# A graph layer with an FFN: half of the FFN up product moved into the first bucket's sums, half between the down products

## The chip, the cores and the metric

One core of one Trainium2 chip. The metric is the device time in microseconds of one execution, the median of several runs. The kernel is written instruction by instruction: each engine has its own program, and semaphores order them against each other.

## The reference

6250 nodes with 256 features (fp32) and 106250 edges. In short:

```
xn = layernorm(x)
low  = relu(segment_sum(val_low[:, None]  * (xn @ W_low)[src],  dst))
high = relu(segment_sum(val_high[:, None] * (xn @ W_high)[src], dst))
mlp  = relu(xn @ W_mlp)
att  = softmax(sigmoid([low @ a0, high @ a1, mlp @ a2]) @ A / 3)
x1   = x + 3 * (att0 * low + att1 * high + att2 * mlp) + mix(xn)
x2   = layernorm(x1)
w    = x2 @ wr + br
y    = gelu(x2 @ w1 + b1) @ w2 + b2        # 256 -> 1024 -> 256
out  = x1 + x2 + (w is among the top 3124) * w * y
```

The kernel sums the node features over the edges first and multiplies by the weights W_low and W_high afterwards. `mix` is a linear attention with an MLP; it is done before the part that the change touches.

## The kernel before, in words

Up to about 850 us of the trace the kernel sorts the edges by target node, stores the normalized rows in memory and does the mix part. Then comes the loop that matters here, in `pipeline`: 50 stages over T = 49 tiles of 128 nodes, written out (not a loop on the chip). A tile has two buckets of 64 nodes. The sorted edges lie in columns of 128; a column's 128 source rows (256 fp32 each, 128 KB) are gathered from memory by one indirect DMA that GpSimd issues (L665), into a ring of 32 columns (`gring`). There are 852 columns, some 8.7 for a bucket.

A bucket's sums are matmuls on TensorE: `bucket` takes ten columns, five in a first half and five in a second, and in between, by a branch, the extra columns of a bucket that spans more. The stationary operand `msel` is a selection matrix of 128 x 128 that VectorE builds for each half (L1116 and L1122 in `select`), and the moving one is the gathered column (128x256), whose place in the ring is computed at run time. After each half TensorE increments `sel_used`. SyncE waits for `sel_used` values (L562) and frees the ring's columns in groups of 8 (`col_free`, L564); GpSimd issues the gathers of a group when it is freed.

In stage i TensorE works on several tiles at once (function `stage` of the tensor block), in this order: transposes of the sums of tile i-1 (L1817), the bias of the down product of tile i-3, transposes of the normalized tile i-2 (L1827), the product with the two GNN weights for tile i-1, the first bucket of tile i into bank 0, down for tile i-3 (eight matmuls of 128x256 into bank 7, then `y_psum`), up for tile i-2 (sixteen of 128x128, banks 4 and 5, `f1_psum` after each eight), and the second bucket of tile i into bank 1. Nearly all matmuls are recorded at L1528, the helper `mm`. An fp32 matmul of the source appears as two weight loads and two matmuls in the trace.

The other engines in a stage. ScalarE: the copy of bank 1 (L1443, releases the next stage's transposes), the copies of the transposes (L1447), the GNN product (L1452), the transposed tile (L1456, sets `x2t_ready`), then the copy of bank 0 (L1490), which waits for the second half of the first bucket, then the attention (L1460, L1462), the reciprocal square root, the scaling of y (L1481, waits for `y_psum`) and the gelus (L1438, wait for `f1_psum`). VectorE, in its program's order: the end of tile i-2, the selection matrices of the first bucket, the attention and layer norm of tile i-1 (`post_a`, L1164 to L1197), and only then the selection matrices of the second bucket. `post_a` waits for the attention's first tanh on ScalarE (L1460), which stands behind L1490:

```
if here:
    act.wait_ge(S("sel_used"), 4 * i + 2)
    act.activation(agg[:, 0, :], bank[0][:, 0:D], ACT.Copy).then_inc(S("agg_a"), 1)
if before1:
    attention(i)
```

Of the kernel before, what the change touches and what calls it, by code (L numbers as in the profile page):

```python
# [22 lines left out]
P = 128  # L23
# [27 lines left out]
def build(nc, a, out):  # L51
# [6 lines left out]
    KD = D // P  # L58
# [40 lines left out]
    with ExitStack() as ctx:  # L99
        sems = {}  # L100

        def S(name):
            if name not in sems:
                sems[name] = ctx.enter_context(nc.semaphore(name))
            return sems[name]
# [1420 lines left out]
        def _(pe):  # L1526
            def mm(out_, lhsT, rhs, start, stop, **kw):
                return pe.matmul(out_, lhsT, rhs, start=start, stop=stop, **kw)  # L1528
# [241 lines left out]
            def add_col(acc, weights, col, start, stop):  # L1770

                at = pe.snap((col % GR) * D)
                return mm(acc[:, 0:D], weights, rows[:, ds(at, D)], start, stop, skip_group_check=True)

            def bucket(b, acc):

                word = bucket_word(pe, b)
                lo = first_col(pe, word)
                more = extra_cols(pe, word)
                pe.wait_ge(S("g_ready"), pe.snap(lo + VIS))  # L1780
                pe.wait_ge(S("sel_ready"), 2 * b + 1)
                for j in range(VIS):
                    ins = add_col(acc, msel[:, 2 * b % NBUF, j, :], lo + j, j == 0, False)
                ins.then_inc(S("sel_used"), 1)
                with pe.If(more > 0):
                    done = extras_so_far(pe, b)
                    with pe.Fori(0, more) as e:
                        pe.wait_ge(S("g_ready"), pe.snap(lo + e + VIS + 1))
                        pe.wait_ge(S("sel_x_ready"), pe.snap(done + e + 1))
                        add_col(acc, msel_x[:, :], lo + e + VIS, False, False).then_inc(S("sel_x_used"), 1)  # L1790
                rest = pe.snap(lo + more)
                pe.wait_ge(S("g_ready"), pe.snap(rest + BOTH))
                pe.wait_ge(S("sel_ready"), 2 * b + 2)
                for j in range(VIS):
                    ins = add_col(acc, msel[:, (2 * b + 1) % NBUF, j, :], rest + VIS + j, False, j == VIS - 1)
                ins.then_inc(S("sel_used"), 1)

            def up(part):

                for f in range(part * KF // 2, (part + 1) * KF // 2):  # L1800
                    for k in range(KD):
                        ins = mm(bank[4 + part][:, (f % 4) * P:(f % 4 + 1) * P], w1f[:, k, f * P:(f + 1) * P], x2t[:, k, :],
                                 k == 0, k == KD - 1)
                return ins

            def down(lo, hi):

# [4 lines left out]
            def stage(i, here, before1, before2, before3):  # L1812
# [24 lines left out]
                    ins.then_inc(S("lh_psum"), 1)  # L1837
                if here:
                    wait(pe, S("agg_a"), i)
                    bucket(2 * i, bank[0])  # L1840
                if before3:
                    down(0, KF).then_inc(S("y_psum"), 1)
                if before2:
                    if isinstance(i, int) and i == 2:
                        pe.wait_ge(S("ffn_loaded"), 16 * 2)
                    pe.wait_ge(S("x2t_ready"), i - 1)
                    for part in range(2):
                        up(part).then_inc(S("f1_psum"), 1)
                if here:
                    wait(pe, S("agg_b"), i)  # L1850
                    bucket(2 * i + 1, bank[1])
# [11 lines left out]
            def end():  # L1863
# [7 lines left out]
                down(0, KF).then_inc(S("y_psum"), 1)  # L1871
                count_total(0)
                pe.wait_ge(S("x2t_ready"), T)
                up(0).then_inc(S("f1_psum"), 1)
                count_total(1)
                up(1).then_inc(S("f1_psum"), 1)
                count_total(2)
                down_bias(T - 1)
                pe.wait_ge(S("fh_ready"), T * KF)
# [36 lines left out]
```

## Time and profile before

| | |
|---|---|
| median of 3 runs | 2526.34 us |
| lowest, highest run | 2504.72, 2528.77 us |
| span of the profiled execution | 2481.7 us |
| its own time around the span | not on the page |
| TensorE busy | 1719.4 us, 69% of the span |
| GpSimd, VectorE, ScalarE busy | 1371.7, 1229.1, 924.8 us |
| gathers from the node rows (L665) | 852 |

The page has the busy time by engine, the span in 40 slices, the DMA queues, the chain of work that ended last, and the costliest groups of instructions by line. Below it the trace answers for single stretches: a timeline has one row for a run of like instructions, with its start, its length, how many, and the idle time before it with what ended that. "issue" stands for no releaser known, "remote" for one that the profile cannot name. Four stages of the loop are looked at, each from its L1817 transposes to the next one's: stage A from 1476.31 us, B from 1384.57, C from 1535.19, D from 2299.98.

### The profile page before, as it was taken

To read this page: it belongs to the slowest core of one execution; us is meant where nothing else is said; L and a number is where in the kernel's file an instruction comes from. 1 tells how busy PE (TensorE), PEld (TensorE's weight loads), DVE (VectorE), ACT (ScalarE), POOL (GpSimd) and SP (SyncE) were. 2 spreads that over 40 slices of the span, in tenths; PEclk is the share of its full clock that TensorE was granted. 3 is DMA by queue.
4 is the path that set the end of the run, shared out by engine and by line. 5 is a ranking of instruction groups with operands and counts; after the bars stand their busy time and mean duration, and the time that the engine had idled before them with its cause. 6 is when DMAs were issued, how large, how long until landed. Compare 5 with 4: busy or idle time off the path is not lost.

```text
span 2481.7 us, 30518 instructions
## 1 busy us (share of the span) xinstructions
PE 1719.4 (69%) x9109; PEld 1441.9 (58%) x9109; DVE 1229.1 (50%) x3164; ACT 924.8 (37%) x2641; POOL 1371.7 (55%) x1351
## 2 busy tenths in 40 slices
PE   4788884998865347776777677677577677667672
PEld 4566673887754335665665666566466566556562
DVE  8899995888761223432343333333333333333336
ACT  2677873777652112321222222222222222222223
POOL 3277675788776565545555455455455545554600
PEclk9899996999967667888887888788788788788886
DMA  3221211111100422222222222222222222222303
GB/s 90 72 63 54 80 33 30 46 54 46 46 5 5 133 85 72 78 69 75 71 74 71 68 73 75 65 72 75 68 73 75 75 69 71 81 71 68 85 9 104
DMA packets 102212, 162.99 MB, mean 66 GB/s; under 512 B 32190, under 2 KB 72762, under 8 KB 102040
## 3 DMA queue, kind: packets, MB, share of 16 engines
q0 software_dynamic: 55232, 113.59, 16.4%
q1 hardware_dynamic: 46808, 47.29, 6.0%
q8 instruction: 85, 1.39, 0.2%
q14 instruction: 87, 0.71, 0.1%
HBM read 139.76 MB, written 21.04 MB: 65 GB/s over the span
## 4 chain that ended last, share of the span: by engine, by line
PE 51%; issue 23%; DVE 10%; ACT 9%; another core or an unknown queue 5%; DMA 1%; SPq 1%; POOL 0%; DVEq 0%; ACTq 0%; POOLq 0%
PE bank L1528 49%; ACT side L1303 2%; PE bank L1817 1%; ACT base L1303 1%; ACT arena L1303 1%; DVE arena L811 1%; ACT arena L1447 1%; ACT arena L1443 1%; DVE arena L733 1%; ACT side L1519 1%; DVE arena L766 1%; ACT arena L1307 0%; PE bank L1602 0%; DVE arena L781 0%
## 5 line engine op out<-in xcount | busy, mean ns | idle before, releaser
L1528 PE MATMUL bank<-arena 128*128 128x128 f32 (+3 forms) x6320 | 1292.5, 359 | 508.2 <-issue 426.8
L1528 PEld LDWEIGHTS bank<-arena 128*128 128x128 f32 (+1 forms) x6320 | 1094.8, 205 | 683.8 <-issue 500.0
L665 POOL DMA_INDIRECT arena<-xn_rows,arena x852 | 825.5, 969 | 733.8 <-SPq L564 450.0
L648 POOL DMA_INDIRECT sorted_records<-arena x448 | 523.0, 1167 | 256.0 <-issue 139.3
L1167 DVE CUSTOM_DVE_ANT_0 arena<-arena 128x256 f32<-128x256 f32 x98 | 37.8, 423 | 414.9 <-ACT arena L1452 376.1
L1122 DVE TENSOR_TENSOR arena<-arena 128x640 f32<-128x640 bf16 (+1 forms) x204 | 164.2, 805 | 47.6 <-DVE arena L1116 17.7
L1172 DVE SCALAR_TENSOR_TENSOR att_prod<-sg,att_neg 128x9 f32<-128x9 f32 x49 | 8.5, 174 | 334.9 <-issue 300.8
L1490 ACT ACTIVATE arena<-bank 128x256 f32<-128x256 f32 x49 | 18.8, 383 | 355.5 <-remote 262.1
L1116 DVE SCALAR_TENSOR_TENSOR arena<-io,arena 128x320 bf16<-128x320 f32 (+1 forms) x204 | 97.8, 479 | 106.3 <-DVE wall L1209 43.5
L1528 PE MATMUL bank<-arena,base 128*128 128x128 f32 (+3 forms) x766 | 118.4, 287 | 16.7 <-ACT base L1307 8.3
L1438 ACT ACTIVATE arena<-bank,b1f 128x128 f32<-128x128 f32 x392 | 110.3, 372 | 33.5 <-PE bank L1528 28.1
L811 DVE TENSOR_TENSOR arena<-arena 128x1280 f32<-128x1280 bf16 x84 | 120.5, 1488 | 4.1 <-remote 1.7
L1528 PEld LDWEIGHTS bank<-arena,base 128*128 128x128 f32 (+2 forms) x766 | 110.2, 211 | 17.6 <-ACT base L1307 8.5
L1443 ACT ACTIVATE arena<-bank 128x256 f32<-128x256 f32 x49 | 18.8, 383 | 247.0 <-PE bank L1528 219.3
L1528 PE MATMUL bank<-side,arena 128*128 128x512 f32 x196 | 97.1, 619 | 0.3 <-issue 0.3
L1481 ACT ACTIVATE side<-bank,wall 128x256 f32<-128x256 f32 x49 | 23.1, 472 | 176.0 <-remote 165.3
L1303 ACT ACTIVATE base<-arena 128x128 f32<-128x128 f32 x280 | 84.7, 391 | 9.4 <-DVE arena L792 9.4
L1468 ACT ACTIVATE nr<-nri 128x1 f32<-128x1 f32 x49 | 9.9, 203 | 206.0 <-issue 159.8
L1303 ACT ACTIVATE arena<-arena 128x128 f32<-128x128 f32 x280 | 84.6, 397 | 0.0
L1303 ACT ACTIVATE side<-arena 128x128 f32<-128x128 f32 x280 | 84.6, 392 | 0.0
L1528 PE MATMUL bank<-arena,side 128*128 128x128 f32 x560 | 73.5, 282 | 12.0 <-issue 10.9
L1528 PEld LDWEIGHTS bank<-arena,side 128*128 128x128 f32 x560 | 68.0, 196 | 15.6 <-issue 14.1
(312 smaller groups left out, 1889.2 us busy)
## 6 DMA issues: line engine op xcount, KB each, us to landing
arena<-xn_rows,arena POOLq DMA_INDIRECT x852
sorted_records<-arena POOLq DMA_INDIRECT x448
arena<-in_x SPq DMA_DIRECT2D x12, 512.0 KB
xn_rows<-arena SPq DMA_DIRECT2D x12, 512.0 KB
x_plus_xn_rows<-arena SPq DMA_DIRECT2D x12, 512.0 KB
arena<-x_plus_xn_rows SPq DMA_DIRECT2D x12, 512.0 KB
arena<-xn_rows SPq DMA_DIRECT2D x12, 512.0 KB
out<-base SPq DMA_DIRECT2D x4, 1024.0 KB
```

Of the source, the lines that this page charges most:

```text
L648: pool.indirect_dma_start(rec_dram, bass.IndirectOffsetOnAxis(ap=idx[0:PR, par, u:u + 1], axis=0), stage_rec[0:PR, par, u * 8:(u + 1) * 8] ...
L665: pool.indirect_dma_start(gring[:, c % GR, :], None, xn_dram, bass.IndirectOffsetOnAxis(ap=rring[:, c, 3:4].bitcast(I32), axis=0)).then_in ...
L733: ins = dve.tensor_tensor(oh[:, t, :].rearrange("p j (h e) -> p j h e", e=2), twice[:, t, :].unsqueeze(2).to_broadcast([P, GS, NB // 2, 2] ...
L766: dve.tensor_tensor(prod4[:, :, :, 0:NB], oh[:, :, :].rearrange("p (s j) b -> p s j b", s=GROUPS), rankf[:, :].rearrange("p (s b) -> p s b ...
L811: dve.tensor_tensor(cellrec[:, t, :].rearrange("p t (f c) -> p t f c", f=4), cell[:, t, :].unsqueeze(2).to_broadcast([P, GS, 4, GC]), raw[ ...
L1116: return dve.scalar_tensor_tensor(out_, io64[:, :].unsqueeze(1).to_broadcast([P, n, BK]), float(BK * b), r[:, :, 0:1].to_broadcast([P, n, ...
L1122: return dve.tensor_tensor(out_, hots.unsqueeze(2).to_broadcast([P, n, 2, BK]), r[:, :, 1:3].unsqueeze(3).to_broadcast([P, n, 2, BK]), ALU ...
L1167: ins = dve.tensor_tensor_reduce(out=lg_prod[:, k, :], in0=lh[:, k * D:(k + 1) * D], in1=att_rows[:, k, :], scale=1.0, scalar=0.0, op0=ALU ...
L1303: ins = act.activation(quot[:, j, :], iota32[:, :], ACT.Abs, bias=p32[:, par, s * GS + j:s * GS + j + 1], scale=-1.0)
L1438: act.activation(fh[:, f, :], bank[4 + part][:, (f % 4) * P:(f % 4 + 1) * P], ACT.Gelu_apprx_tanh, bias=b1f[:, f:f + 1]).then_inc(S("fh_re ...
L1443: act.activation(agg[:, 1, :], bank[1][:, 0:D], ACT.Copy).then_inc(S("agg_b"), 1)
L1528: return pe.matmul(out_, lhsT, rhs, start=start, stop=stop, **kw)
```

## The change

The up product of a stage is cut into blocks: `up_block(f)` is the two matmuls of the hidden block f, and after every fourth it increments `f1_psum`. Blocks 0 to 3 are issued inside the second half of the first bucket, one ahead of each of its first four columns. The waits for the transposed tile (and, in stage 2, for the FFN weights) stand ahead of them, in the bucket. Blocks 4 to 7 alternate with the eight matmuls of down: a block, two of down, and so on. `y_psum` still comes after the last of down. In the stages without a bucket (the last one) all blocks alternate with down. The last tile's end is the same but for where `f1_psum` is written down in the source.

```
             def bucket(b, acc, turned=0):
...
                 pe.wait_ge(S("sel_ready"), 2 * b + 2)
+                if turned == 1:
+                    pe.wait_ge(S("ffn_loaded"), 16 * 2)
+                if turned:
+                    pe.wait_ge(S("x2t_ready"), turned)
                 for j in range(VIS):
+                    if turned and j < KF // 2:
+                        up_block(j)
                     ins = add_col(acc, msel[:, (2 * b + 1) % NBUF, j, :], rest + VIS + j, False, j == VIS - 1)
                 ins.then_inc(S("sel_used"), 1)

+            def up_block(f):
+
+                for k in range(KD):
+                    ins = mm(bank[4 + f // 4][:, (f % 4) * P:(f % 4 + 1) * P], w1f[:, k, f * P:(f + 1) * P], x2t[:, k, :],
+                             k == 0, k == KD - 1)
+                if f % 4 == 3:
+                    ins.then_inc(S("f1_psum"), 1)
...
                 if here:
                     wait(pe, S("agg_a"), i)
-                    bucket(2 * i, bank[0])
+                    bucket(2 * i, bank[0], i - 1 if before2 else 0)
+                elif before2:
+                    pe.wait_ge(S("x2t_ready"), i - 1)
+                for f in range(KF):
+                    if before2 and (not here or f % 2 == 0):
+                        up_block(KF // 2 + f // 2 if here else f)
+                    if before3:
+                        ins = down(f, f + 1)
                 if before3:
-                    down(0, KF).then_inc(S("y_psum"), 1)
-                if before2:
-                    if isinstance(i, int) and i == 2:
-                        pe.wait_ge(S("ffn_loaded"), 16 * 2)
-                    pe.wait_ge(S("x2t_ready"), i - 1)
-                    for part in range(2):
-                        up(part).then_inc(S("f1_psum"), 1)
+                    ins.then_inc(S("y_psum"), 1)
```

How TensorE's row changes, from the second half of the first bucket on, in a middle stage (bank0: the first bucket's sums, bank7: down, bank4 and bank5: up, ISA: the register work for a column's place). Before:

```order
L1792 ISA
L1528 ISA [waits sel_ready,g_ready]
L1528 MATMUL bank0<-arena 128x256
L1528 ISA
L1528 MATMUL bank0<-arena 128x256
L1528 ISA
L1528 MATMUL bank0<-arena 128x256
L1528 ISA
L1528 MATMUL bank0<-arena 128x256
L1528 ISA
L1528 MATMUL bank0<-arena 128x256
L1528 MATMUL bank7<-arena 128x256 x8
```

and now:

```order
L1792 ISA
L1528 MATMUL bank4<-arena 128x128 [waits x2t_ready,sel_ready,g_ready]
L1528 MATMUL bank4<-arena 128x128
L1528 ISA
L1528 MATMUL bank0<-arena 128x256
L1528 MATMUL bank4<-arena 128x128 x2
L1528 ISA
L1528 MATMUL bank0<-arena 128x256
L1528 MATMUL bank4<-arena 128x128 x2
L1528 ISA
L1528 MATMUL bank0<-arena 128x256
L1528 MATMUL bank4<-arena 128x128 x2
```

The eight short matmuls into bank 4 now stand between the columns of bank 0, so the last column's matmul, which increments `sel_used`, has them ahead of it.

Then the row up to the second bucket (TENSOR_LOAD of `packed` is its first instruction). Before:

```order
L1528 MATMUL bank0<-arena 128x256
L1528 MATMUL bank7<-arena 128x256 x8
L1528 MATMUL bank4<-arena 128x128 [waits x2t_ready]
L1528 MATMUL bank4<-arena 128x128 x7
L1528 MATMUL bank5<-arena 128x128 x8
L406 TENSOR_LOAD packed [waits agg_b]
```

and now:

```order
L1528 ISA
L1528 MATMUL bank0<-arena 128x256
L1528 MATMUL bank5<-arena 128x128 x2
L1528 MATMUL bank7<-arena 128x256 x2
L1528 MATMUL bank5<-arena 128x128 x2
L1528 MATMUL bank7<-arena 128x256 x2
L1528 MATMUL bank5<-arena 128x128 x2
L1528 MATMUL bank7<-arena 128x256 x2
L1528 MATMUL bank5<-arena 128x128 x2
L1528 MATMUL bank7<-arena 128x256 x2
L406 TENSOR_LOAD packed [waits agg_b]
```

The down products into bank 7 come later by the short ones between them, and the last instructions ahead of the second bucket are two of down, not eight of up.

## Rows read from the trace of the kernel before

**Rows 1.** The page: busy time by engine, and the chain that ended last.

```profile
PE 1719.4 (69%) x9109; PEld 1441.9 (58%) x9109; DVE 1229.1 (50%) x3164; ACT 924.8 (37%) x2641; POOL 1371.7 (55%) x1351
...
PE 51%; issue 23%; DVE 10%; ACT 9%; another core or an unknown queue 5%; DMA 1%; SPq 1%; POOL 0%; DVEq 0%; ACTq 0%; POOLq 0%
```

**Rows 2.** Waits from 1100 to 2300 us: us in total, times, longest us.

```profile
POOL arena L665 <- SPq L564: 371.7, 53, 13.1
...
PE bank L1528 <- issue: 326.4, 247, 3.2
...
ACT arena L1490 <- remote: 194.7, 24, 11.1
```

**Rows 3.** Groups by shape from 1100 to 2300 us: busy us, mean ns, idle before.

```profile
L1528 PE MATMUL bank<-arena 128*128 128x128 f32 x1216 | 236.3, 328 | 328.1 <-issue 324.9 <-DVE arena L1122 2.5
```

**Rows 4.** Timeline of TensorE in stage A: start us, length us, records, idle before.

```profile
1476.31 0.66 PE L1817 MATMUL bank<-ident,arena 128*128 128x128 f32 x4 [0.47 <-ACT arena L1443]
...
1477.72 11.95 PE L1528 MATMUL bank<-arena 128*128 128x256 f32 x61 [0.42 <-ACT arena L1447]
1490.40 0.40 PE L1528 MATMUL bank<-arena 128*128 128x128 f32 x2 [0.73 <-issue]
...
1497.55 6.98 PE L1528 MATMUL bank<-arena 128*128 128x128 f32 x29 [0.38 <-issue]
```

**Rows 5.** Timeline of GpSimd around stage A.

```profile
1474.65 0.94 POOL L665 DMA_INDIRECT arena<-xn_rows,arena  x1 [9.12 <-SPq L564]
...
1485.56 0.94 POOL L665 DMA_INDIRECT arena<-xn_rows,arena  x1 [1.09 <-issue]
...
1494.43 0.95 POOL L665 DMA_INDIRECT arena<-xn_rows,arena  x1 [0.30 <-issue]
```

**Rows 6.** Stage D, timelines of TensorE, GpSimd, ScalarE and VectorE.

```profile
2301.39 13.34 PE L1528 MATMUL bank<-arena 128*128 128x256 f32 x76 [0.42 <-ACT arena L1447]
2319.27 6.27 PE L1528 MATMUL bank<-arena 128*128 x20 [4.55 <-DVE arena L1122]
2326.01 0.66 PE L1817 MATMUL bank<-ident,arena 128*128 128x128 f32 x4 [0.47 <-ACT arena L1443]
...
2309.24 0.94 POOL L665 DMA_INDIRECT arena<-xn_rows,arena  x1 [1.10 <-issue]
2311.85 0.94 POOL L665 DMA_INDIRECT arena<-xn_rows,arena  x1 [1.67 <-issue]
...
2311.21 0.38 ACT L1490 ACTIVATE arena<-bank 128x256 f32<-128x256 f32 x1 [6.92 <-remote]
...
2318.08 0.88 DVE L1122 TENSOR_TENSOR arena<-arena 128x640 f32<-128x640 bf16 x1
```

**Rows 7.** Stretches: stage A, stage C, stage D (us, then busy us and count by engine).

```profile
1476.31:1505.00 28.69, 21.87 (x103) 18.47 (x104) 11.29 (x37) 7.98 (x26) 14.95 (x16) 0.88 0.26 75
1535.19:1575.93 40.74, 23.65 (x104) 19.67 (x104) 11.52 (x37) 7.98 (x26) 22.00 (x23) 0.75 0.27 78
2299.98:2326.01 26.03, 20.59 (x104) 17.65 (x104) 11.43 (x37) 7.76 (x26) 15.26 (x17) 0.93 0.29 82
```

**Rows 8.** Timeline of ScalarE: L1490 and L1481 in stage A, and L1490 in C.

```profile
1488.99 0.38 ACT L1490 ACTIVATE arena<-bank 128x256 f32<-128x256 f32 x1 [8.37 <-remote]
...
1497.71 0.47 ACT L1481 ACTIVATE side<-bank,wall 128x256 f32<-128x256 f32 x1 [0.25 <-remote]
...
1550.63 0.38 ACT L1490 ACTIVATE arena<-bank 128x256 f32<-128x256 f32 x1 [11.13 <-remote]
```

**Rows 9.** Records of L1528 started in A and in C until L1490 started.

```profile
1477.60:1488.95 11.35, 11.21 (x57) 9.89 (x58) 1.00 0.36 102
1536.50:1550.58 14.08, 11.66 (x58) 10.15 (x58) 1.00 0.37 106
```

**Rows 10.** Stage B: ScalarE's copy, and GpSimd's ninth gather.

```profile
1393.64 0.38 ACT L1490 ACTIVATE arena<-bank 128x256 f32<-128x256 f32 x1 [4.77 <-PE bank L1528]
...
1395.18 0.94 POOL L665 DMA_INDIRECT arena<-xn_rows,arena  x1 [0.30 <-issue]
```

More of the change, by code:

```diff
@@ L1773, in add_col, with bucket @@
                 return mm(acc[:, 0:D], weights, rows[:, ds(at, D)], start, stop, skip_group_check=True)
-            def bucket(b, acc):
+            def bucket(b, acc, turned=0):
                 word = bucket_word(pe, b)
@@ L1793, in bucket @@
                 pe.wait_ge(S("sel_ready"), 2 * b + 2)
+                if turned == 1:
+                    pe.wait_ge(S("ffn_loaded"), 16 * 2)
+                if turned:
+                    pe.wait_ge(S("x2t_ready"), turned)
                 for j in range(VIS):
+                    if turned and j < KF // 2:
+                        up_block(j)
                     ins = add_col(acc, msel[:, (2 * b + 1) % NBUF, j, :], rest + VIS + j, False, j == VIS - 1)
                 ins.then_inc(S("sel_used"), 1)
+            def up_block(f):
[4 more added lines that the diff above has]
+                    ins.then_inc(S("f1_psum"), 1)
             def up(part):
                 for f in range(part * KF // 2, (part + 1) * KF // 2):
[L1801 to L1804, printed above, removed]
+                    up_block(f)
             def down(lo, hi):
@@ L1873, in end @@
                 pe.wait_ge(S("x2t_ready"), T)
-                up(0).then_inc(S("f1_psum"), 1)
+                up(0)
                 count_total(1)
-                up(1).then_inc(S("f1_psum"), 1)
+                up(1)
                 count_total(2)
```

## The prediction

> **What bounds the kernel now.** I read the page first [rows 1]: TensorE is busy 69% of the span, but 23% of the chain that ended last is "issue", time in which an engine waited for nothing the profile names. Then the waits of the 1,200 us stretch 1100 to 2300 us, which holds some 38 stages of the loop over node tiles [rows 2]: TensorE stands 326.4 us on "issue", in 247 pieces, while GpSimd, which issues the gathers, waits 371.7 us for SyncE's releases. Then the groups by shape [rows 3]: nearly all of TensorE's 326.4 us stand in front of the 128x128 matmuls, the FFN up product, in which the program has no wait after the first. So the place that the change touches is the place where the engine stands.
>
> Why does it stand there? I took single stages. One record of a weight load with one of a matmul I call a pair; each fp32 matmul of the source is two pairs. A stage has 7 small ones (four transposes, the bias, two transposes), then 96 pairs: 8 of the product with the GNN weights, 10 and 10 of the first bucket's two halves, 16 of down, 32 of up, 20 of the second bucket. In stage A (1476.31 to 1505.00) 61 of the 96 start in one run, then six trickle in over some 7 us, and the last 29 run again from 1497.55 [rows 4]. GpSimd's gathers of this stage run from 1474.65 to 1495.38 (1494.43 + 0.95), 16 of them, one each 1.25 us, with a break of 1.09 us after the eighth [rows 5]. TensorE comes free 2.2 us after the last of them. In stage D the gathers had a break at 2310.2 to 2311.85; TensorE ran 76 pairs without a stop, and the stage took 26.0 us instead of 28.7 [rows 6, 7].
>
> The messages of TensorE tell more. The copy of the first bucket's sums (ScalarE L1490) waits for the second half's last matmul, pair 28; in the stretch it waits 194.7 us for a releaser that the profile can't name ("remote") [rows 2]. That pair starts some 7.3 us into a stage (1.4 us, and 27 times 0.22), yet L1490 starts at 1488.99 in stage A (12.7 us in) and at 1550.63 in stage C (15.4 us in) [rows 8]. I counted what TensorE had started by then: 57 matmuls and 58 weight loads in A, 58 and 58 in C [rows 9], though the two moments are 2.7 us apart in their stages. So while gathers run, the completion of a pair is reported only when about 30 further pairs have started: completions leave in order, one for each instruction, and slowly. The scaling of the down product (L1481) says the same: it waits for pair 44, which starts at 10.8 us in, and starts at 1497.71, just after TensorE came free [rows 8]. In stage D, with the break, L1490 starts 1.0 us after the gather before the break ended [rows 6]. Why the completions are held is not in the trace; that they are, and in which order, is.
>
> The second thing to see is what hangs on L1490. It is followed by the attention, VectorE's chain for the tile and only then VectorE's selection matrices for the second bucket, since VectorE keeps its program order. In stage D: L1490 at 2311.21, selection ready at 2318.96, second bucket from 2319.27 [rows 6]: 8.1 us. From there 6.7 us to the next stage's transposes (2326.01). So where this chain decides, a stage ends 14.8 us after L1490 (20 pairs in 6.27 us is the rate at a granted clock near 1.2 GHz, TensorE having stood; at 0.22 us each, as in the run of 76, it would be 1.9 less). In stage A this chain needs 1497.1, and TensorE comes to the second bucket at some 1499.4: hidden, by 2.3 us.
>
> **The change, part by part.** Instructions are neither added nor taken away: the same 32 up pairs, moved; no DMA, no other engine's code. (a) Half of up, 16 pairs, goes into the second half of the first bucket. The wait for the transposed tile moves ahead of it; that copy lands 3.9 us into a stage, and the half begins at 5.3: nothing. (b) The other half stands between the down pairs. Pure order, except for what stands behind TensorE's release: of the 8 pairs then left, 4 are now of 256 columns instead of 128. At 6.27 us for 20 such pairs [rows 6] that is 0.31 each, 0.16 more than a half-wide one, 0.6 us a stage. (c) The message that L1490 waits for now sits on pair 44 instead of 28. Without any hold that is 16 short pairs later, 1.8 us (13.34 us for 76 pairs of which 32 are half as wide [rows 6]: 0.22 us for a wide one, 0.11 for a short one). With the hold it is the whole matter: pair 44 is where the down product's message sat, and that one never came through before the gathers ended. By the count, TensorE would have to start 74 pairs for it, and it has 67 when it is released (96 less the 29 of the last run [rows 4]).
>
> So L1490 moves to the end of the gathers, or to their first break. There are four kinds of stage among the 45 from the third on. A stage begins with its four transposes (L1817); the counts are from the timeline of GpSimd's gathers, by the number in a burst, its start in the stage and what released each group of 8:
> - 23 like A: both groups released by earlier halves. L1490 at 21.2 after the stage's start (1497.55 less 1476.31), stage 21.2 + 14.8 = 36.0. Before, their mean is 29.2 (A 28.7 [rows 7]): +6.8 each, +156.
> - 4 with the same releases but gathers from 0.5 to 20.6 in: L1490 at 23.4, stage 38.2 against 30.9: +29.
> - 11 like B: the second group of 8 is released by this very message (L1490 at 1393.64, the ninth gather at 1395.18 [rows 10]). Now GpSimd runs dry at 10.5 in, the break lets the completions out as in stage D, after 1.0 us, or 2.2 as at a burst's end; I take 1.6, near the middle. L1490 at 12.1, stage 26.9 against 31.0: -4.1 each, -45.
> - 7 like C: 24 gathers, the last 8 released by this message. The break comes at 18.4, L1490 at 20.6, stage 35.4 against 40.7 [rows 7]: -5.3 each, -37.
>
> Sum: 156 + 29 - 45 - 37 = +103 us on the profiled execution's span of 2481.7. Its own time around the span isn't on the page; the lowest of the three runs, 2504.72, is 23 above it, the median 44.6. I add the difference to the median: 2526 + 103 = 2629, say 2630. (b) isn't added, since TensorE then waits for VectorE anyway. Bounds of the uncertain terms: if pair 44's message came as early as pair 28's plus 1.8 us, the first two kinds cost 0.6 us each or +17; if the two dry kinds save nothing, the sum is +185; if the second bucket ran at the quick rate in the 27 slower stages, it is 51 less, +52.
>
> On the hold itself a page speaks against me. The Trainium skill, "SBUF — State Buffer", section "SBUF: two separate sides", says that engine ports and DMA ports are disjoint and that a DMA can't be slowed by a compute operation or the other way round. By that rule the gathers wouldn't hold TensorE, the message would move by 1.8 us alone, and the sum would be that of the first rival; the break of stage D and TensorE's release 2.2 us after the gathers speak for a link, if not through these ports.
>
> **Rivals.**
> First: the message moves with its instruction, by some 2 us, and nothing more. Then L1490 is at 14.5 in stage A, the second bucket could start at 22.6, where TensorE arrives at 23.1: still hidden, and only (b) is paid: 45 x 0.6 = 27 us, 2553. For it: in B and stages like it, pair 28's message came within 2 us. Against it: 58 pairs in both A and C, and the down message, which was never early.
> Second, on the other side: the dry GpSimd wins. In the 18 stages of the last two kinds the break is worth 82 us; if in the other 27 the message of pair 44 comes by about 15 us into the stage (15 + 8.1 is where TensorE arrives now), these lose only 0.6 us each. 2526 - 82 + 17 = 2461. It decides on whether pair 44 can be reported before some 62 pairs have started. For it: the break after the eighth gather in A did come while completions were held; against it: pair 28 had been done by then and still wasn't reported until 1488.99.
> Third: the interleaving evens out TensorE's rate and the hold never builds up. Then all stages go like D, near 27: 45 stages at a mean of 31.6 before would give some 2320. Against it: the number of pairs is the same, and the run of 61 ended in the same place in stages whose gathers began 2 us apart.
>
> **Chances.** The forecast 0.52. First rival 0.20, at +27 us just on the border of 1% (1% is about what a measurement of this kernel can tell from no change), so half of it counts as the same. Second 0.19, third 0.04, the rest (a mixture that cancels, near zero) 0.05. Faster 0.24, same 0.16, slower 0.60. The range leaves the third rival and the very worst out: 2455 to 2700.
>
> **What would show it.** In the changed kernel's trace: L1490 starting 20 us and more into most stages, just after TensorE's release, where L1481 starts now; the second bucket waiting for VectorE L1122 by some 5 us, a wait that the profile then names; TensorE's "issue" time about as large as before in stages like A, and gone in stages like B, which shrink to 27; stages like C at 35. Wrong, if L1490 starts at 13 to 15 in stages like A: then the count of 30 pairs is no rule. Wrong the other way, if more than 70 pairs start before the gathers end.

## The result: slower, and the profile after

The changed kernel takes 2622.22 us in the median (2607.58 to 2635.47, four runs); the kernel before 2527.56 (2504.72 to 2559.39, four runs, three of them those of the table above). The ratio is 1.0483, with a 95% interval from 1.0438 to 1.0527. Two further sets of the unaltered changed kernel gave 1.0468 and 1.0438 (below). Where several runs of a kernel lie in two groups, the ratios and intervals here and below are those of the faster group, so that they can differ from the quotient of the medians.

The page of the profiled execution (2607.58 us, span 2605.8), the busy times and the chain that ended last, which answer to [rows 1]:

```profile
PE 1785.5 (69%) x9109; PEld 1446.8 (56%) x9109; DVE 1230.7 (47%) x3164; ACT 915.3 (35%) x2641; POOL 1378.3 (53%) x1351
...
PE 34%; another core or an unknown queue 21%; issue 14%; DVE 13%; POOL 9%; ACT 7%; DVEq 1%; DMA 1%; SPq 0%; ACTq 0%; POOLq 0%
```

The counts are the same on every engine. The chain has shifted: TensorE from 51% to 34%, "issue" from 23% to 14%, and "another core or an unknown queue", which is what the profile writes for a message that it can't attribute, from 5% to 21%. Two groups of the page say which message. Before:

```profile
L1172 DVE SCALAR_TENSOR_TENSOR att_prod<-sg,att_neg 128x9 f32<-128x9 f32 x49 | 8.5, 174 | 334.9 <-issue 300.8
...
L1490 ACT ACTIVATE arena<-bank 128x256 f32<-128x256 f32 x49 | 18.8, 383 | 355.5 <-remote 262.1
```

and now:

```profile
L1172 DVE SCALAR_TENSOR_TENSOR att_prod<-sg,att_neg 128x9 f32<-128x9 f32 x49 | 8.3, 170 | 647.1 <-ACT sg L1460 586.2
L1490 ACT ACTIVATE arena<-bank 128x256 f32<-128x256 f32 x49 | 18.8, 383 | 677.4 <-remote 667.7
```

ScalarE stands 677.4 us in front of the copy of the first bucket (355.5 before), and VectorE 647.1 us for the attention behind it (334.9): 49 copies of 0.38 us are what the stage waits for. The waits of the stretch 1100 to 2400 us (us in total, times, longest us), which answer to [rows 2]; it is 100 us longer than the stretch there, and holds as many stages, some 38:

```profile
ACT arena L1490 <- remote: 532.3, 38, 19.0
DVE att_prod L1172 <- ACT sg L1460: 474.4, 33, 18.9
...
PE bank L1528 <- issue: 226.4, 200, 6.0
...
PE bank L1528 <- DVE arena L1122: 136.7, 23, 7.0
```

The wait for the unnamed releaser went from 194.7 us in 24 pieces to 532.3 in 38. TensorE's "issue" became smaller, 326.4 to 226.4, and beside it there is now a wait with a name, 136.7 us for VectorE's L1122, the selection matrices of the second bucket; it was 2.5 us [rows 3]. TensorE still stands inside its own products, but less, and now it also waits for the chain.

A stage like A, from 1548.68 to 1585.75. TensorE, then ScalarE, then GpSimd, as timelines (start us, length us, records, idle before); they answer to [rows 4, 5 and 8]:

```profile
1548.68 0.66 PE L1828 MATMUL bank<-ident,arena 128*128 128x128 f32 x4 [0.47 <-ACT arena L1443]
...
1550.08 11.05 PE L1528 MATMUL bank<-arena 128*128 128x256 f32 x63 [0.42 <-issue]
...
1568.21 3.06 PE L1528 MATMUL bank<-arena 128*128 128x128 f32 x6 [0.34 <-issue]
1577.65 7.63 PE L1528 MATMUL bank<-arena 128*128 x20 [6.37 <-DVE arena L1122]
1585.75 0.66 PE L1828 MATMUL bank<-ident,arena 128*128 128x128 f32 x4 [0.47 <-ACT arena L1443]
```

```profile
1569.66 0.38 ACT L1490 ACTIVATE arena<-bank 128x256 f32<-128x256 f32 x1 [16.67 <-remote]
```

```profile
1554.65 0.94 POOL L665 DMA_INDIRECT arena<-xn_rows,arena  x1 [0.30 <-SPq L564]
...
1565.90 0.95 POOL L665 DMA_INDIRECT arena<-xn_rows,arena  x1 [0.30 <-issue]
1583.24 1.35 POOL L665 DMA_INDIRECT arena<-xn_rows,arena  x1 [16.39 <-SPq L564]
```

63 pairs in one run, a trickle while the gathers go on, the last gather done at 1566.85, TensorE free at 1568.21, the copy at 1569.66, 21.0 us after the stage's start. From the copy 8.0 us to the second bucket, and TensorE has stood 6.37 us by then. GpSimd in turn stands 16.39 us, since its columns are freed by the same halves.

A stage like B, from 1446.31 to 1473.87, which answers to [rows 10]:

```profile
1447.71 13.34 PE L1528 MATMUL bank<-arena 128*128 128x256 f32 x76 [0.42 <-ACT arena L1447]
1466.52 6.88 PE L1528 MATMUL bank<-arena 128*128 x20 [5.47 <-issue]
...
1458.34 0.38 ACT L1490 ACTIVATE arena<-bank 128x256 f32<-128x256 f32 x1 [7.72 <-remote]
...
1455.67 0.94 POOL L665 DMA_INDIRECT arena<-xn_rows,arena  x1 [0.30 <-issue]
1459.27 0.94 POOL L665 DMA_INDIRECT arena<-xn_rows,arena  x1 [2.65 <-SPq L564]
```

Here GpSimd runs dry at 1456.61, 10.3 us in; the copy comes 1.7 us later, and TensorE runs 76 pairs without a stop. The three kinds as stretches (length us; busy us and count of PE, PEld, DVE, ACT, POOL; granted clock; DMA share; GB/s), against [rows 7]:

```profile
1446.30:1473.91 27.61, 21.24 (x104) 17.98 (x104) 11.57 (x37) 7.76 (x26) 15.93 (x16) 0.88 0.28 77
1548.70:1585.70 37.00, 24.55 (x103) 19.31 (x103) 11.29 (x37) 7.76 (x26) 15.23 (x16) 0.77 0.21 60
1623.30:1658.80 35.50, 23.68 (x103) 18.92 (x104) 11.48 (x37) 7.76 (x26) 22.20 (x23) 0.76 0.30 87
```

The 45 stages together: from the third stage's transposes to the 48th's, in the kernel before and in the changed one:

```profile
945.45 0.66 PE L1817 MATMUL bank<-ident,arena 128*128 128x128 f32 x4 [0.47 <-ACT arena L1443]
...
2367.28 0.66 PE L1817 MATMUL bank<-ident,arena 128*128 128x128 f32 x4 [0.47 <-ACT arena L1443]
```

```profile
961.96 0.66 PE L1828 MATMUL bank<-ident,arena 128*128 128x128 f32 x4 [0.47 <-ACT arena L1443]
...
2483.86 0.66 PE L1828 MATMUL bank<-ident,arena 128*128 128x128 f32 x4 [0.47 <-ACT arena L1443]
```

1421.8 us before, 1521.9 now: +100.1. The rest of the difference of the two spans, 24 us, lies outside these stages. 18.1 of it has come together by the loop's first transposes (889.91 us before, 908.04 now), where the change moves nothing. 7.6 lies behind the 48th stage's transposes (114.4 to 122.0 us), where the last stages and the last tile still carry the change. The first two stages are 1.6 us shorter.

### The profile page after: what moved, and what is told of

It reads as the page before. It is cut to its first block, busy times and chain, and to the rows that moved or that the text cites. A ratio compares the mean times of both kernels' runs of the same rounds, so it can differ in the third digit from the quotient of the medians.

```text
span 2605.8 us, 30518 instructions
## 1 busy us (share of the span) xinstructions
PE 1785.5 (69%) x9109; PEld 1446.8 (56%) x9109; DVE 1230.7 (47%) x3164; ACT 915.3 (35%) x2641; POOL 1378.3 (53%) x1351
## 3 DMA queue, kind: packets, MB, share of 16 engines
q0 software_dynamic: 55232, 113.59, 15.7%
## 4 chain that ended last, share of the span: by engine, by line
PE 34%; another core or an unknown queue 21%; issue 14%; DVE 13%; POOL 9%; ACT 7%; DVEq 1%; DMA 1%; SPq 0%; ACTq 0%; POOLq 0%
PE bank L1528 32%; POOL sorted_records L648 9%; PE bank L1828 1%; DVE arena L1122 1%; ACT arena L1443 1%; ACT arena L1452 1%; ACT side L1519 1%; ACT arena L1447 1%; DVE arena L1116 1%; DVE arena L811 1%; DVE arena L1189 1%; DVE ybuf L1187 1%; DVE arena L1186 1%; ACT side L1303 1%
## 5 line engine op out<-in xcount | busy, mean ns | idle before, releaser
L1528 PE MATMUL bank<-arena 128*128 128x128 f32 (+3 forms) x6320 | 1359.1, 370 | 559.0 <-issue 312.5
L1528 PEld LDWEIGHTS bank<-arena 128*128 128x128 f32 (+1 forms) x6320 | 1100.2, 207 | 798.9 <-issue 604.5
L665 POOL DMA_INDIRECT arena<-xn_rows,arena x852 | 833.9, 979 | 828.1 <-SPq L564 553.0
L1172 DVE SCALAR_TENSOR_TENSOR att_prod<-sg,att_neg 128x9 f32<-128x9 f32 x49 | 8.3, 170 | 647.1 <-ACT sg L1460 586.2
L1490 ACT ACTIVATE arena<-bank 128x256 f32<-128x256 f32 x49 | 18.8, 383 | 677.4 <-remote 667.7
L1122 DVE TENSOR_TENSOR arena<-arena 128x640 f32<-128x640 bf16 (+1 forms) x204 | 164.0, 804 | 31.8 <-DVE arena L1116 3.2
L1528 PE MATMUL bank<-arena,base 128*128 128x128 f32 (+3 forms) x766 | 116.8, 285 | 26.0 <-ACT base L1307 17.0
L1528 PEld LDWEIGHTS bank<-arena,base 128*128 128x128 f32 (+2 forms) x766 | 108.7, 209 | 26.7 <-ACT base L1307 17.5
L1528 PE MATMUL bank<-side,arena 128*128 128x512 f32 x196 | 97.5, 621 | 0.3 <-issue 0.3
L1528 PE MATMUL bank<-arena,side 128*128 128x128 f32 x560 | 74.1, 283 | 12.7 <-issue 12.3
L1528 PEld LDWEIGHTS bank<-arena,side 128*128 128x128 f32 x560 | 68.8, 198 | 15.2 <-issue 14.8
L766 DVE TENSOR_TENSOR arena<-arena 128x2940 f16<-128x2940 bf16 x28 | 47.3, 1689 | 58.5 <-issue 46.4
```

The costliest lines, as they stand in the source:

```text
L665: pool.indirect_dma_start(gring[:, c % GR, :], None, xn_dram, bass.IndirectOffsetOnAxis(ap=rring[:, c, 3:4].bitcast(I32), axis=0)).then_in ...
L766: dve.tensor_tensor(prod4[:, :, :, 0:NB], oh[:, :, :].rearrange("p (s j) b -> p s j b", s=GROUPS), rankf[:, :].rearrange("p (s b) -> p s b ...
L1122: return dve.tensor_tensor(out_, hots.unsqueeze(2).to_broadcast([P, n, 2, BK]), r[:, :, 1:3].unsqueeze(3).to_broadcast([P, n, 2, BK]), ALU ...
```

## The experiments

Eight kernels of my own, two of them run twice, and the changed kernel two times more. The first four ran beside the same 14 runs of the kernel before.

### One half of the move at a time

`e1_bucket_half_only` keeps blocks 0 to 3 inside the bucket and puts down back in one piece, the other blocks behind it:

```
                 for f in range(KF):
-                    if before2 and (not here or f % 2 == 0):
-                        up_block(KF // 2 + f // 2 if here else f)
-                    if before3:
-                        ins = down(f, f + 1)
...
+                    ins = down(0, KF)
                     ins.then_inc(S("y_psum"), 1)
+                if before2:
+                    for f in range(KF // 2 if here else 0, KF):
+                        up_block(f)
```

> Half of up inside the first bucket as in the changed kernel, the other half behind down as before. Theory (the message of pair 44 leaves only when the gathers stop, and the stage ends 14.8 us after it): this half alone is the whole loss, 2600 to 2640 us, L1490 about 21 us into stages like A. Rival (the interleaving of up with down, or of short and wide matmuls, costs): near 2530.

Measured: 2605.81 us (2585.84 to 2653.16), the kernel before beside it 2507.95 (14 runs): 1.0367, interval 1.0279 to 1.0456. The waits of 1100 to 2400 us:

```profile
ACT arena L1490 <- remote: 533.8, 38, 19.0
...
PE bank L1528 <- DVE arena L1122: 150.8, 23, 7.4
```

The wait at L1490 is that of the whole change, 533.8 against 532.3 us. The half in the bucket alone makes the long stages, as expected.

`e2_down_half_only` is the other half: nothing in the bucket, blocks 0 to 3 right behind it, then the alternation with down.

```
-                    bucket(2 * i, bank[0], i - 1 if before2 else 0)
+                    bucket(2 * i, bank[0])
...
+                    if here:
+                        for f in range(KF // 2):
+                            up_block(f)
```

> Nothing inside the bucket: the first half of up behind it, the second half between the down products. Theory: L1490 keeps pair 28 and starts at about 12.7 us in stages like A, stages as long as before, 2520 to 2560 us. Rival (interleaving costs): 2580 and more.

Measured: 2530.51 us (2515.44 to 2539.74): 1.0129, interval 1.0066 to 1.0193. A stage of the kind of A:

```profile
1480.65 10.35 PE L1528 MATMUL bank<-arena 128*128 128x256 f32 x57 [0.42 <-ACT arena L1447]
...
1498.99 9.91 PE L1528 MATMUL bank<-arena 128*128 128x256 f32 x30 [0.83 <-issue]
1509.37 0.66 PE L1822 MATMUL bank<-ident,arena 128*128 128x128 f32 x4 [0.47 <-ACT arena L1443]
...
1491.88 0.38 ACT L1490 ACTIVATE arena<-bank 128x256 f32<-128x256 f32 x1 [8.33 <-remote]
```

L1490 comes 12.6 us into the stage (12.7 in stage A before), but what is left when TensorE is released, 30 pairs with wide ones among them, takes 9.91 us where it took 6.98 for 29 [rows 4]. Over the 45 stages it is 1454.7 us, 32.9 more than before, 0.7 a stage. That is near the 0.6 a stage of the prediction's part (b), but in this stage it isn't made of part (b)'s wide pairs alone: the run of 30 went at a granted clock of 0.66, the 29 of stage A at 0.79, and it began 19.8 us into the stage, not 21.2. So the alternation costs little, as forecast; that the four wide pairs are what it costs isn't shown.

### How far the message may move

`e3_one_block` leaves one block in the bucket, `e4_two_blocks` two; the others stand behind down. The message that L1490 waits for is then on pair 32 and on pair 36, after 28 in the kernel before and 44 in the changed one.

```
-                    if turned and j < KF // 2:
+                    if turned and j < 1:
```

> One block (4 pairs) inside the bucket, seven behind down: the message is on pair 32. Theory: it leaves when about 62 pairs have started, some 13.3 us in, which is still hidden; 2520 to 2560 us. Rival (anything between the columns costs in proportion to its pairs): a quarter of the loss, 2550.

> Two blocks (8 pairs) inside the bucket: the message is on pair 36. Theory: it needs some 66 started pairs and so leaves just before or at the end of the gathers in stages like A, 18 to 21 us in; most of the loss is there already, 2570 to 2620 us. Rival (in proportion): half of the loss, 2575. The place of L1490 tells them apart: at 18 to 21 against 13 to 15 us.

Measured: e3 2519.59 us (2468.62 to 2549.33, ten runs), 0.9945, interval 0.9867 to 1.0024. e4 2528.22 us (2487.48 to 2584.41, four runs), for which there is no interval: no verdict, though its slowest run is still below the fastest of the changed kernel's in any set, 2594.67. The 2570 to 2620 expected of e4 was wrong, and for the rival's 2575 there is no sign either. Their profiled executions took 2549.28 and 2531.61 us, so only what happens within their stages is read from them. The copy in a stage of the kind of A of e3, and the run of TensorE around it:

```profile
1272.10 0.38 ACT L1490 ACTIVATE arena<-bank 128x256 f32<-128x256 f32 x1 [9.83 <-remote]
...
1259.37 11.86 PE L1528 MATMUL bank<-arena 128*128 128x256 f32 x61 [0.42 <-ACT arena L1447]
```

and in e4:

```profile
1295.94 0.39 ACT L1490 ACTIVATE arena<-bank 128x256 f32<-128x256 f32 x1 [11.90 <-remote]
...
1304.10 6.05 PE L1528 MATMUL bank<-arena 128*128 x20 [1.99 <-DVE arena L1122]
```

The stages begin at 1257.97 and 1279.73. So the copy comes 12.7 us into such a stage with the message on pair 28, 14.1 on 32, 16.2 on 36, 21.0 on 44: 1.4 us for the first four pairs, 2.1 for the next four, 4.8 for the last eight. Sixteen pairs more at the rate of the free run, 0.175 us a pair, would be 2.8 us; they are 8.3. And it is not steady: of the 23 stages of this kind, five in e3 and nine in e4 have their copy at 19.6 to 21.2 us, and in the changed kernel 21 of them at 20.6 to 22.3. The later the message stands, the more often it falls behind the last gather. The expectation for e4, the copy at 18 to 21 us in stages like A, so holds for fewer than half of them. In e4, 10 of the 45 stages are of 27.0 to 27.7 us, those in which GpSimd runs dry, which pays for some of the long ones.

One number is the same in all four places of the message. Over the 45 stages of each kernel, at most 59 pairs had started when the copy did with the message on pair 28, 63 with it on pair 32, 67 on 36 and 75 on 44: 31 behind it each time.

### Does a break in the gathers let the completions out?

The next four kernels were made for that. `e5` and `e6` are the changed kernel and the one before with a single edit in SyncE's program, which rounds the count of used passes up to an even number, so that groups of 8 are freed later:

```
-                        used = sp.snap(word % 256, min_val=1, max_val=255)
+                        used = sp.snap((word % 256 + 1) // 2 * 2, min_val=2, max_val=256)
```

`e7` is e6, and SyncE also waits until TensorE has come to the up product of a stage (its first matmul increments `paced`; in the first two stages, which have no up product, the first matmul of the second bucket does), so that the gathers must break in each stage:

```
+                        sp.wait_ge(S("paced"), sp.snap((used + 2) // 4, min_val=1, max_val=64))
...
+                        if tell and f == 0 and k == 0:
+                            ins.then_inc(S("paced"), 1)
```

`e8` is the kernel before, with gathers of a quarter of each row (64 of 256 features; the other three quarters of the ring stay zero, so it sums something else), which moves a quarter of the bytes with the same instructions:

```
-                    gring[:, c % GR, :], None, xn_dram,
+                    gring[:, c % GR, 0:D // 4], None, xn_dram.rearrange("n (k d) -> (n k) d", k=4),
```

> The changed kernel, but SyncE frees the columns only when a whole bucket (both halves) has been summed: its wait value is rounded up to an even number. So GpSimd runs dry in every stage until the first bucket's message. Theory (completions leave when the gathers break): stages like A become like B, 27 us instead of 36, L1490 at 12; only stages with three groups stay long; 2330 to 2450 us, faster than both. Rival (the late message has nothing to do with the gathers running): later gathers can only cost, 2620 to 2700.

> The kernel before with the same rounding. The first bucket's message is on pair 28 and comes before the first 8 gathers are issued, so there is no break. Theory: all stages go like B of the kernel before, 31 us, those with three groups 40: 2550 to 2620 us. Rival (the rounding itself helps): clearly under 2500.

> The kernel before with the rounding, and the release that hangs on the first bucket waits for the first up matmul (pair 45) as well. The message for L1490 stays on pair 28. Theory: L1490 at 8 to 10 us, a break of GpSimd at about 10.5 us in until pair 45 is reported, no trickle, stages of 24 to 27 us: 2200 to 2350 us. Rival (gathers don't hold TensorE): 2550 and more, since the gathers start later.

> The kernel before, each gather fetching 256 bytes for an index instead of 1 KB (other rows than asked for; the sums are not the reference's). GpSimd issues as many gathers at the same pace, with a quarter of the bytes. If the bytes hold TensorE's completions, the trickle is gone: 2300 to 2400 us. If the issuing of gathers (descriptors) does, all is as before: 2500 to 2560.

Measured, all of it unlike what either theory said: the kernel before itself took 1985.86 us here (1979.68 to 1989.94, 25 runs), some 500 less than in every run until then. e5: 2082.94 us, 1.0497 (1.0475 to 1.0519). e6: 1986.5, 1.0000 (0.9990 to 1.0010). e7: 1985.01, 1.0003 (0.9993 to 1.0012). e8: 1985.52, 1.0003 (0.9989 to 1.0016).

In these runs completions aren't held. A stage of e6, from 1101.43:

```profile
1102.83 13.34 PE L1528 MATMUL bank<-arena 128*128 128x256 f32 x76 [0.42 <-ACT arena L1447]
1117.16 2.42 PE L1528 MATMUL bank<-arena 128*128 x10 [0.99 <-DVE arena L1122]
1120.85 2.42 PE L1528 MATMUL bank<-arena 128*128 x10 [1.26 <-SPq L554]
...
1109.18 0.38 ACT L1490 ACTIVATE arena<-bank 128x256 f32<-128x256 f32 x1 [3.44 <-PE bank L1528]
```

The gathers go on through the whole of it, one each 1.25 us. The copy comes at 7.8 us, its releaser has a name, and by 1109.15 TensorE had started 29 pairs, not 58 as in [rows 9]:

```profile
1102.30:1109.15 6.85, 6.32 (x29) 5.60 (x30) 1.00 0.35 98
```

What bounds this state is GpSimd: for 1000 to 1900 us its groups have (busy us, mean ns, idle before)

```profile
L665 POOL DMA_INDIRECT arena<-xn_rows,arena x683 | 681.8, 998 | 208.1 <-issue 197.4 <-SPq L564 10.7
```

683 gathers in 900 us with 10.7 us of waiting. Most of them follow each other at 1.25 us, some later, 1.30 in the mean. A stage in which TensorE doesn't wait for gathered columns takes 20.8 us, but the 774 gathers that are issued in the 45 stages need 1007.6 us, 22.4 a stage. e8 tells that it is their issuing and not their bytes: 29.84 MB in place of 113.59 go through the gathers' queue, at the same pace and in the same time. e7 had no breaks here: GpSimd waited for SyncE by 0.3 us at most, 2.7 in all between 1000 and 1900 us, since the message it waits for came in time. So it doesn't tell what a break costs without a hold.

The change loses just as much here, by another road. A stage of e5, from 1130.26:

```profile
1131.66 13.34 PE L1528 MATMUL bank<-arena 128*128 128x256 f32 x76 [0.41 <-ACT arena L1447]
1147.79 6.26 PE L1528 MATMUL bank<-arena 128*128 x20 [2.79 <-DVE arena L1122]
1154.53 0.65 PE L1828 MATMUL bank<-ident,arena 128*128 128x128 f32 x4 [0.47 <-ACT arena L1443]
...
1139.80 0.38 ACT L1490 ACTIVATE arena<-bank 128x256 f32<-128x256 f32 x1 [5.23 <-PE bank L1528]
```

The copy comes at 9.5 us instead of 7.8, which is the distance of 16 short pairs that the prediction gives (1.8 us). With no hold the chain behind it isn't hidden: TensorE already waited 0.99 us for VectorE in e6, and now waits 2.79. After that longer pause its granted clock is lower. The stretches of the second bucket in e5 and in e6 (the clock is the third number from the end), and the second bucket of e6's stage before, which didn't wait for columns in its middle:

```profile
1147.79:1154.05 6.26, 6.26 (x20) 4.84 (x20) 4.53 (x11) 2.88 (x11) 2.89 (x3) 0.73 0.25 77
```

```profile
1117.16:1119.58 2.42, 2.42 (x10) 1.81 (x10) 1.88 (x5) 2.39 (x10) 1.95 (x2) 1.00 0.27 81
```

```profile
1096.38 4.58 PE L1528 MATMUL bank<-arena 128*128 x20 [0.99 <-DVE arena L1122]
```

20 pairs take 6.26 us at 0.73 where they take 4.58 at 1.00: 1.7 us more. 1.7 of message and 1.7 of clock make a stage of 24.3 us out of one of 20.8, which is above the 22.4 that the gathers need: 1098.0 against 1007.6 us over the 45 stages, +90. e5 carries the rounding too. e6 shows it to be worth nothing in the kernel before, and in e5's 45 stages TensorE never waits for a gathered column, so it isn't what bounds e5 either.

### The same with the hold

The two that mattered were run again, `e9_after_again` (the changed kernel unaltered) and `e10_before_paced_again` (the kernel of e7).

> The changed kernel once more, since the kernel before took 1986 us on the chip of the last four runs against 2508 to 2528 on the two before: there TensorE's completions weren't held. Theory for a chip with the hold: 1.04 to 1.05 as before. For a chip without it: L1490 starts 1.8 us later in a stage, but the gathers (852 at 1.25 us) set the pace and the 8.1 us chain behind L1490 fits beside them: 0.99 to 1.02. Rival (the change costs something of its own, as the 1.05 of the run with whole passes may be read): 1.03 to 1.06 without any hold too.

> The paced kernel once more. On a chip with the hold, theory: GpSimd's break at about 10.5 us into each stage lets the completions out, stages of 24 to 27 us, 2200 to 2350 us. Rival (gathers don't hold TensorE): 2550 and more. On a chip without it: the same as the kernel before, as in the run already made.

Measured: the hold was there again, the kernel before took 2494.94 us (2489.18 to 2545.64, seven runs). e9: 2624.26 us (2609.92 to 2674.47), 1.0468 (1.0404 to 1.0533). e10: 2316.91 us (2304.04 to 2332.62), 0.9261 (0.9202 to 0.9321), the fastest kernel with the hold in this study, and within the 2200 to 2350 expected. A stage of e10, from 1352.46 to 1377.81 (L1492 is the copy there, L667 the gather):

```profile
1361.72 0.38 ACT L1492 ACTIVATE arena<-bank 128x256 f32<-128x256 f32 x1 [4.95 <-remote]
...
1353.87 13.34 PE L1530 MATMUL bank<-arena 128*128 128x256 f32 x76 [0.41 <-ACT arena L1449]
1369.70 4.58 PE L1530 MATMUL bank<-arena 128*128 x20 [2.49 <-DVE arena L1124]
...
1361.88 0.95 POOL L667 DMA_INDIRECT arena<-xn_rows,arena  x1 [0.30 <-issue]
1365.69 0.96 POOL L667 DMA_INDIRECT arena<-xn_rows,arena  x1 [2.87 <-SPq L566]
```

GpSimd now breaks for 2.87 us after the eighth gather and again at the stage's end, TensorE runs 76 pairs without a stop, and the copy comes at 9.3 us. That is ahead of the break in the stage; the one before it, 2.99 us up to 1353.14, spans the stage's start. The 45 stages take 1248.3 us, 173.5 less than before, with as many gathers, and the granted clock over them is 0.89 in place of 0.83. Two things remain open. The kernel carries the rounding of e6 too, and e6 was never run with the hold, so what the rounding alone gives there isn't known. And e10 holds back gathers and nothing else, so it shows that their timing decides when TensorE's completions get through, but not by what path.

`e11_quarter_rows_again` (the kernel of e8) was to ask whether bytes or issuing hold the completions:

> The kernel before with 256 bytes an index once more (other rows than asked for), since the first such run fell on a chip without the hold, where it said nothing. On a chip with it: if the bytes that the gathers move hold the completions, no trickle, stages of 22 to 26 us, 2050 to 2350 us. If the number of gathers and of their descriptors does, stages as before with L1490 at 12 to 13 us in stages like A, 2480 to 2560 us.

Measured: no hold again, the kernel before 1985.79 us (13 runs), e11 1985.1, 0.9995 (0.9983 to 1.0007). The question stays open.

`e12_changed_third_time` is the changed kernel once more, for the case that the hold were absent:

> The changed kernel, unaltered, a third time. What is open is whether the change also costs time on a run in which TensorE's completions are not held back by the gathers. If the kernel before takes about 2500 us beside it, the hold is there, and both theories expect what was measured twice: a ratio of 1.04 to 1.055, about 2610 to 2640 us. If the kernel before takes about 1986 us, the hold is absent. The theory that the whole loss comes from the hold then expects 0.995 to 1.01 (1975 to 2005 us): GpSimd sets the pace with its gathers, and a message that leaves 1.7 us later is hidden behind them in most stages. The rival, that a later message costs its own delay in every stage whatever the hold, expects what the run with an even count of issued passes gave there, 1.04 to 1.055 (2065 to 2095 us): 45 stages by about 2 us.

Measured: the hold was there. 2627.96 us (2594.67 to 2635.21) against 2501.34 (2490.0 to 2509.5, seven runs), 1.0438 (1.0345 to 1.0530). It repeats the result; that the unaltered changed kernel loses without a hold too rests on e5 against e6.

## Why the prediction was right, point by point

2630 us was forecast, with slower as the likeliest; 2622.22 was measured. The forecast for the stages was +103 us on the profiled execution; they took +100.1. That it comes so near is in part luck: three stages that the prediction took for long ones were short, 26 us less in sum, and the other 42 took 24 us more than forecast. The kinds of stage, with the same counts (11 in which GpSimd's second group hangs on the message, 7 of 24 gathers, 4 with gathers from 0.5 us in, 23 others), forecast and measured mean of a stage:

| kind | forecast | measured | change, forecast | change, measured |
|---|---|---|---|---|
| 23 like A | 36.0 | 35.7 | +156 | +149 |
| 4 with a later start | 38.2 | 35.7 | +29 | +19 |
| 11 like B | 26.9 | 27.4 | -45 | -40 |
| 7 like C | 35.4 | 36.7 | -37 | -28 |

**The copy moves to the end of the gathers or to their first break.** Right: 21.0 us in at 1548.68 (21.2 forecast), 12.0 in stages like B (12.1), 20.5 to 21.6 in those like C (20.6). (For the four with a later start the prediction has 23.4 where its own terms, 20.6 and 2.2, give 22.8; that is 2 us of the sum.) e1 shows that this part alone does it, e3 and e4 how it sets in.

**A stage ends 14.8 us after the copy.** Nearly. The 8.1 us to the second bucket were 8.0, but its 20 pairs took 6.88 and 7.63 us and not 6.27; the mean from the copy to the stage's end over the 45 is 15.5. The prediction takes the 6.27 us of stage D for the rate at a granted clock near 1.2 GHz; that stretch (2319.27 to 2325.54) was granted 0.73 in the mean, which is neither of the two levels throughout, so there was room below it. The 20 pairs took 4.58 us at 1.00 after 2.49 us of standing (e10), 6.26 at 0.73 after 2.79 (e5), 6.27 at 0.73 after 4.55 (stage D), 6.88 at 0.66 after 5.47 (1466.52), and after the 6.37 us here 0.59:

```profile
1577.72:1585.10 7.38, 7.38 (x20) 5.79 (x20) 4.76 (x12) 2.80 (x11) 1.35 (x1) 0.59 0.02 4
```

**A completion is reported only when about 30 more pairs have started.** As a bound this held, as a fixed count it did not. When the copy started, between 57 and 75 pairs of a stage had started, which is 13 to 31 behind pair 44; 58 were 30 behind pair 28 [rows 9]. So the message never was more than 31 pairs late, but where the gathers broke it came after fewer. A bound of that sort, the same 31 in four places of the message, can also be read the other way round: TensorE may be unable to start more than 31 pairs beyond the last one reported, and then its "issue" time is the consequence of the late reports. No run here separates the two readings. The prediction also named more than 70 pairs before the end of the gathers as a sign against it; 8 of the 45 stages have 71 to 73. The copy came late in them all the same, 1.5 to 2.9 us after the last gather, so the count alone didn't bring it. The Trainium skill, "TensorE: Matmul & The Clock Gate", gives the engine a queue of 64 entries in the table under the title. With a weight load and a matmul for each pair that is, as an estimate from the page's figure, 32 pairs, and the bound of 31 agrees with it. No run here varies the depth of the queue.

**In stages like B the break lets it out.** Right: 1.7 us after the eighth gather was done, forecast 1.6. Breaks in the gathers are also what e10 adds on purpose. Three stages of the other kinds (29.9, 27.3 and 26.8 us, forecast at 38 and 36) had their copy at 11.4 to 11.7 us in as well; most of what the table has too low for the second kind is one of them.

**Part (b) isn't added.** Right where it was used, since TensorE waits for VectorE's L1122 in the long stages (136.7 us). Alone the other half costs 1.3% (e2, 0.7 us a stage), near the 0.6 us a stage, though the clock had a part in it.

**The time around the span.** The prediction took 23 to 44.6 us for what lies between the span of the profiled execution and a run's time. It is 1.8 us (2607.58 less 2605.8). The profiled execution of before was a quick one, 18 us of it ahead of the loop against the changed kernel's, and the median stood 1.8% above its span for that reason. It made no error in the sum, since the difference was added to the median.

**The rivals.** The first (the message moves by its 1.8 us, which stays hidden, +1%) has its mechanism in e5, right in its size (1.7), but with the wrong consequence: without a hold the chain isn't hidden, and the later message costs 90 us together with the lower clock that follows it. It took the cover of stage A, where TensorE came late to the second bucket because it was held, as a cover for the case in which it isn't. The second (the dry GpSimd wins) was a quarter true: stages like B and C do get shorter, by 68 us in sum, which the others more than take back. The third did not occur.

**The page against the hold.** The Trainium skill, "SBUF — State Buffer", section "SBUF: two separate sides", has it that a DMA can't slow a compute operation. The runs without a hold agree: gathers without a pause, TensorE's 76 pairs in 13.34 us, the copy at 7.8. The held ones have the same 13.34 us for 76 pairs as long as it may run on; what is late in them is the report of a completion, and perhaps through it TensorE's further starts, on which that rule says nothing.

## What to carry to other kernels

A matmul moved ahead of the one that carries a message delays the whole chain behind that message, and what it costs is read from who waits at its end: find the message's instruction, count what now stands ahead of it, and follow the waits to the next thing TensorE itself needs. Work put into a gap of TensorE's belongs behind such a message and not in front of it. A cover that consists of an engine being late is no cover if the cause of its lateness can go away, so work the sum out for the undisturbed stage as well.

## What the runs showed of the hardware that was not expected

The same program took 1986 us in some sets of runs and about 2500 in others, each time steady within a set, and one and the same chip had a set of either sort. The traces show where the 500 us between them lie: 414 us in the 45 stages (1421.8 against e6's 1007.6), 85 ahead of them. In the stages TensorE's completions reach the other engines late while GpSimd issues indirect gathers, with up to 31 pairs between, and with breaks of some 3 us in the gathers the kernel is 7.4% faster (e10). Why a set has it or not isn't in any trace, and neither is whether bytes or issuing matter to it, since both runs with quarter rows fell on sets without it. In the sets without, a quarter of the bytes changed nothing: 1.25 us per indirect gather of 128 rows, from issue to issue (the median; the mean is 1.30), was GpSimd's own pace at 256 and at 1024 bytes a row alike.
